# TensorE drains in the fused attention: who waits for a matmul's own increment, and who for a drain

## The chip, the core and the metric

The program runs on one core of one Trainium2 chip. Its five engines go by short names: PE (TensorE), DVE (VectorE), ACT (ScalarE), POOL (GpSimd) and SP (SyncE). They run their own instruction streams and meet only at semaphores: counters that one engine raises and another waits for. The metric is the device time of one execution in microseconds, the median of the runs shown.

## The reference, cut to what matters

Four graph layers follow one another on 3125 nodes of 256 features and 100,000 edges: an attention layer with two convolutions (L0), a dot-product attention (L1), a layer with edge features (L2), and another attention layer (L3). The change lies in the code that computes a convolution of L0 (twice) and the attention of L3:

```
h = (x @ W).reshape(-1, H, C)                     # H = 4 heads of 64
e = leaky_relu(alpha_s[src] + alpha_d[dst], 0.2)  # one score for an edge and a head
m = segment_max(e, dst);  ex = exp(e - m[dst])
alpha = ex / segment_sum(ex, dst)
out = segment_sum(h[src] * alpha[:, :, None], dst) + b
```

The edges are sorted by the node that receives them, so that each segment is a run of neighbours.

## The kernel before, in words

`attend` (line 1354) runs three times: for L0 with the tags `0a` and `0b`, for L3 without a tag. Tiles are named `at_..._0a`, `at_..._0b` and `at_...`. It takes the edges in units of 128; a turn is 16 units (STEP), in four quads of four (QUAD), and a stage has 51 turns. Every engine runs its own function `step` once a turn. There is no scheduler: instructions stand in the order of the code, and each engine goes down its list, stopping at waits.

A turn of step t, by engine:

- POOL gathers one unit's 128 rows from the node table in HBM with an indirect DMA (L1515), and fills a scratch tile after each one (`pause`, L1519). The ring holds three turns; a quad's gathers wait for that quad's matmuls two steps earlier.
- DVE scales a quad of gathered rows by their weights (`weigh_rows`, L1572); computes the scores (`y` at L1592 to `shrink`, a chain of some 17 short instructions); adds each unit's sums to the node's accumulator (`add`, L1566); and last `factor` (L1652), and at the head of the next step `rescale` (L1582). Its order is: rescale, rows of quad 0, scores, rows of quad 1, add 0 to 3, rows of quad 2, add 4 to 7, rows of quad 3, add 8 to 11, add 12 to 15, factor.
- ACT makes one-hot matrices (`hot`, `hot_r`), the exponents (`exp`), copies the turned exponents out of PSUM as weights (`alphas`, L1810), then `parts` (L1816), and `own` (L1835).
- PE runs scores, mm0 to mm11 (one matmul `mm{u}` for each unit, two passes each in the trace, L1680, into the four banks of `at_po`), 16 small `spread` matmuls (L1692), the exponents' transpose with `back_turned` as its last matmul (L1723, L1724), mm12 to mm15, eight matmuls on scratch (`keep_busy`, L107), and `joined` (L1735), whose result `own` needs.

Each engine has one semaphore that its instructions raise by position: `m.did("mm12", ...)` hangs an increment on the matmul, and `m.at("mm12", t)` is the value that the counter has by then, a register value in the loop. ACT waits before `alphas` at `m.at("back_turned", t)`, and DVE before each `add{u}` at `m.at("mm{u}", t)`. A matmul mm{u} waits for add{u-4}, which frees its bank.

Of the kernel before, what the change touches and what calls it, by code (L numbers as in the profile page):

```python
# [32 lines left out]
QUAD = 4  # L33
# [38 lines left out]
def gnn_kernel(nc, x_in, src_in, dst_in, attr_in, ew_in, W1, as1, ad1, b1, W2, as2, ad2, b2, Wq, bq, Wk, bk, Wv, bv,  # L72
# [30 lines left out]
    def keep_busy(eng, scratch, count):  # L103

        wide = scratch.shape[1] // P
        for _ in range(count):
            eng.matmul(scratch.rearrange("p (k n) -> p k n", n=P), ident16[:, :],  # L107
                       ident16[:, :].rearrange("p (k n) -> p k n", k=1).to_broadcast([P, wide, P]), start=True, stop=True)
# [1245 lines left out]
    def attend(tag, o, table, kind, scatter=0):  # L1354
# [26 lines left out]
        with ExitStack() as c:  # L1381
# [39 lines left out]
            ph = Phase()  # L1421
            vec, act, mat, fed, told, cleared = (ph.sem(n) for n in (
                "at_vector", "at_scalar", "at_tensor", "at_fed", "at_told", "at_cleared"))
# [4 lines left out]
            rows_in = [ph.sem(f"at_rows_in{h}") for h in range(2)]  # L1428
            v, s, m = Ops(vec, V, 3), Ops(act, A, 1), Ops(mat, M, 3)
            paused, blank = ph.sem("at_paused"), ph.sem("at_blank")  # L1430
            moving = Scatter(f"at_{tag}", ph, c, scatter) if scatter else None

            def run(eng, step):

                step(Turn(0, -1), False, False, True)
                step(Turn(0, 0), False, True, True)
                with eng.Fori(0, LAPS - 1) as i:
                    for k in range(1, BUFS + 1):
                        step(Turn(i, k), True, True, True)
                step(Turn(LAPS - 1, 1), True, True, True, True)  # L1440
                step(Turn(LAPS - 1, 2), True, True, False)
                step(Turn(LAPS - 1, 3), True, False, False, True)

            with nc.Block() as block:
# [86 lines left out]
                def _(eng):  # L1531
# [10 lines left out]
                    def step(t, sums, scores, spreads, short=False):  # L1542
# [15 lines left out]
                        def add(*us):  # L1558
                            for u in us:
                                if not sums or u >= quads * QUAD:  # L1560
                                    v.skip(f"add{u}")
                                    continue
                                eng.wait_ge(mat, m.at(f"mm{u}", t))
                                done("rescale" if u < 2 else f"add{u - 2}", t)
                                to = acc2[:, u % 2, bass.ds(gs[u], 1), 0:W]
                                v.did(f"add{u}", eng.tensor_tensor(to, to, po[:, u % 4:u % 4 + 1, 0:W], ALU.add))  # L1566
# [97 lines left out]
                @block.tensor  # L1664
                def _(eng):
                    def step(t, sums, scores, spreads, short=False):
                        a = t.plus(-1)
                        quads = TAIL if short and not scores else STEP // QUAD

                        def reduce(q):  # L1670
                            for j in range(QUAD):
                                u = q * QUAD + j
                                if not sums or q >= quads:
                                    m.skip(f"mm{u}")
                                    continue
                                if j == 0:
                                    eng.wait_ge(vec, v.at(f"rows{q}", t))
                                    eng.wait_ge(act, s.at(f"ext{q}", t))
                                eng.wait_ge(vec, v.at(f"add{u - 4}", t) if u >= 4 else v.at(f"add{u + 12}", a))
                                m.did(f"mm{u}", eng.matmul(po[:, u % 4, 0:W], hot[:, q % 2, j, :],  # L1680
                                                           rows[:, q % 2, j, :, :].rearrange("p h f -> p (h f)"),
                                                           start=True, stop=True))

                        def spread(h, gs):
                            if not spreads:
                                return m.skip(f"spread{h}")
                            eng.wait_ge(act, s.at(f"hot_r{h}", t))
                            if scores and h == 0:
                                eng.wait_ge(act, s.at("parts", a))
                            for k in range(HALF):  # L1690
                                u = h * HALF + k
                                mm = eng.matmul(pb[:, u, :, :].rearrange("p k c -> p (k c)"),  # L1692
                                                hot_r[:, h, k * P:(k + 1) * P],
                                                b_tab[:, bass.ds(gs[u], 1), :, 0:C].rearrange("p o k c -> p (o k) c"),
                                                start=True, stop=True)
                            m.did(f"spread{h}", mm)

                        if scores:
                            eng.wait_ge(act, s.at("picked", a))
                            if sums:  # L1700
                                eng.wait_ge(vec, v.at("y", a))
                            eng.sem_inc(told, 1)
                            m.did("scores", eng.transpose(scores_in, picked[:, :, :].rearrange("p h u -> p (h u)"), ident[:, :]))
                            keep_busy(eng, spare_b, 6)
                        else:
                            m.skip("scores")
                        reduce(0)
                        reduce(1)
                        reduce(2)
                        gs = None  # L1710
                        if spreads:
                            _, gs = nc.values_load_multi_w_load_instructions(
                                od["gof"][0:1, bass.ds((t.n + 1) * STEP, STEP)], engines=[ENG.PE], min_val=0, max_val=NB,
                                skip_runtime_bounds_check_because="the table is clamped to NB on the chip")
                        spread(0, gs)
                        spread(1, gs)
                        if scores:
                            if sums:
                                eng.wait_ge(vec, v.at(f"rows{quads - 1}", t))
                            eng.wait_ge(act, s.at("exp", t))  # L1720
                            eng.sem_inc(told, 1)
                            for k in range(KX):
                                eng.transpose(pe[:, k * R:(k + 1) * R], expd[:, k * P:(k + 1) * P], ident[0:R, 0:R])  # L1723
                            m.did("back_turned", eng.matmul(pe[:, KX * R:KX * R + H],  # L1724
                                                            expd[:, EX:EX + 1].to_broadcast([R, P]), ident[0:R, 0:R:STEP],
                                                            start=True, stop=True))
                        else:
                            m.skip("back_turned")
                        reduce(3)
                        if spreads:  # L1730
                            if scores:
                                keep_busy(eng, spare, 8)
                            eng.wait_ge(act, s.at("parts", t))
                            for k in range(3):
                                mm = eng.matmul(joined[0:C * STEP, :], parts[:, k, :, :].rearrange("p c u -> p (c u)"),  # L1735
                                                ident[:, :], start=(k == 0), stop=(k == 2))
                            m.did("joined", mm)
                        else:
                            m.skip("joined")

                    eng.sem_inc(mat, 2 * len(M))
                    run(eng, step)

                @block.scalar
                def _(eng):
                    done = lambda name, t: eng.wait_ge(act, s.at(name, t))

                    def step(t, sums, scores, spreads, short=False):
# [57 lines left out]
                        if scores:  # L1806
                            if sums and quads == STEP // QUAD:
                                done("ext3", t)
                            eng.wait_ge(mat, m.at("back_turned", t))
                            s.did("alphas", eng.activation(al[:, :, :, :].rearrange("p k h u -> p (k h u)"), pe[:, 0:KX * R],  # L1810
                                                           ACT.Copy))
                        else:
                            s.skip("alphas")
# [24 lines left out]
                        else:  # L1838
                            s.skip("own", *(["selfs"] if own_max else []))

                    run(eng, step)
            ph.end()

# [815 lines left out]
```

## Time and profile before

| | us |
|---|---|
| runs: 3, median | 7405.61 |
| lowest to highest | 7398.5 to 7406.8 |
| the profiled execution: its span, which is the only time it has | 8931.6 |
| POOL, PE, DVE, ACT busy in that span | 5847.5, 5412.5, 4963.7, 3871.5 |

The profiled execution took 1.206 times the median of the runs, so its times can't be taken for those of a plain run without thought. A duration of an ACT, DVE or POOL instruction is measured; a matmul's end is modelled. An engine's idle time before an instruction is shown with what ended it, where the profile can tell. Where it names a DMA of long before (`recs_s<-rnk_recs_now`), it could not tell.

### The profile page before, as it was taken

How to read it: one execution, taken by the hardware profiler on the slowest of the kernel's cores; microseconds unless marked ns; L12 is line 12 of the kernel's file. 1: busy time of each engine (PE TensorE's matmuls, PEld its weight loads, DVE VectorE, ACT ScalarE, POOL GpSimd, SP SyncE). 2: the span in 40 equal slices, each digit the busy share in tenths (PEclk: the TensorE clock that was granted, in tenths of full speed). 3: DMA queues.
4: the chain of work that ended last, by engine and by line, in shares of the span. 5: the costliest groups of instructions: out<-in, count | busy, mean ns of one | idle time of the engine just before them, and what ended most of it. 6: DMA issues, size and time to landing. Idle time of an engine off the chain costs nothing. (4 is left out here: it accounts for less than half of the span.)

```text
span 8931.6 us, 130458 instructions
## 1 busy us (share of the span) xinstructions
PE 5412.5 (61%) x23088; PEld 4000.6 (45%) x23089; DVE 4963.7 (56%) x11653; ACT 3871.5 (43%) x9075; POOL 5847.5 (65%) x8186
## 2 busy tenths in 40 slices
PE   6442365666535656664676666658888754666665
PEld 5431244444424444443455555435555533444443
DVE  6444355555545555554677777744444445555556
ACT  2220255455424554552244444335555533454444
POOL 0555677777747777775467666657777765777774
PEclk9555677777767777776788988868888866777777
DMA  4112233333313333331466666423333323333332
GB/s 143 49 49 52 75 95 95 95 96 95 86 44 97 96 95 95 96 97 33 127 176 178 177 176 175 129 64 99 100 101 100 101 53 101 99 99 99 98 98 74
DMA packets 580940, 894.72 MB, mean 100 GB/s; under 512 B 307359, under 2 KB 357708, under 8 KB 580448
## 3 DMA queue, kind: packets, MB, share of 16 engines
q0 software_dynamic: 245984, 649.30, 26.7%
q1 hardware_dynamic: 334448, 218.84, 8.9%
q10 hardware_dynamic: 416, 25.60, 0.9%
q8 instruction: 27, 0.44, 0.0%
q14 instruction: 65, 0.53, 0.0%
HBM read 859.36 MB, written 59.47 MB: 103 GB/s over the span
## 5 line engine op out<-in xcount | busy, mean ns | idle before, releaser
L2002 POOL DMA_INDIRECT ad_ring<-tab_qv,ad_idx x808 | 770.7, 954 | 506.4 <-issue 217.6
L1515 POOL DMA_INDIRECT at_ring_0a<-tab_s,at_idx_0a x808 | 774.3, 958 | 430.9 <-PE at_po_0a L1680 219.2
L2396 POOL DMA_INDIRECT ae_ring<-tab_a,ae_idx x808 | 777.9, 963 | 423.0 <-PE ae_po L2553 233.7
L1515 POOL DMA_INDIRECT at_ring_0b<-tab_s,at_idx_0b x808 | 772.8, 956 | 426.7 <-PE at_po_0b L1680 213.2
L1515 POOL DMA_INDIRECT at_ring<-tab_s,at_idx x808 | 780.1, 965 | 377.6 <-PE at_po L1680 183.0
L1680 PE MATMUL at_po_0a<-at_rows_0a,at_hot_0a 128*128 128x264 f32 x1616 | 625.6, 560 | 520.8 <-ACT at_hr_0a L1780 199.8
L1680 PE MATMUL at_po_0b<-at_rows_0b,at_hot_0b 128*128 128x264 f32 x1616 | 624.3, 559 | 512.2 <-ACT at_hr_0b L1780 201.7
L1680 PE MATMUL at_po<-at_rows,at_hot 128*128 128x260 f32 x1616 | 614.5, 553 | 444.5 <-DVE acc L1566 179.0
L1680 PEld LDWEIGHTS at_po_0a<-at_rows_0a,at_hot_0a 128*128 128x128 f32 x1616 | 439.3, 282 | 670.8 <-DVE acc L1566 262.0
L1680 PEld LDWEIGHTS at_po_0b<-at_rows_0b,at_hot_0b 128*128 128x128 f32 x1616 | 438.5, 282 | 662.4 <-DVE acc L1566 264.4
L1680 PEld LDWEIGHTS at_po<-at_rows,at_hot 128*128 128x128 f32 x1616 | 435.9, 280 | 586.2 <-DVE acc L1566 225.4
L2182 PE MATMUL ad_pk<-node_a,ad_hr 128*128 x1616 | 485.0, 452 | 337.6 <-issue 193.1
L2546 PE MATMUL ae_pM<-ae_we,ae_featT 64*128 64x256 f32 x1616 | 508.0, 465 | 171.3 <-issue 114.5
L1566 DVE TENSOR_TENSOR acc<-acc,at_po_0a 128x264 f32 x808 | 314.0, 422 | 483.9 <-PE at_po_0a L1680 215.1
L1566 DVE TENSOR_TENSOR acc<-acc,at_po_0b 128x264 f32 x808 | 312.9, 422 | 481.5 <-PE at_po_0b L1680 212.2
L566 POOL DMA_INDIRECT recs_s<-rnk_recs_now,rnk_pos_now x294 | 288.8, 982 | 409.9 <-DVE rnk_both L466 176.2
L2182 PEld LDWEIGHTS ad_pk<-node_a,ad_hr 128*128 128x128 f32 x1616 | 350.6, 226 | 452.2 <-issue 396.8
L1566 DVE TENSOR_TENSOR acc<-acc,at_po 128x260 f32 x808 | 307.1, 418 | 437.7 <-DMA recs_s<-rnk_recs_now,rnk_pos_now 178.8
L2553 PE MATMUL ae_po<-ae_msg,ae_hot 128*128 128x256 f32 x1616 | 464.8, 439 | 98.1 <-issue 60.9
L2506 DVE TENSOR_TENSOR ae_pre<-ae_ring,ae_pM 128x1024 f32<-128x1024 f32 x202 | 246.6, 1221 | 493.4 <-PE ae_pM L2546 187.7
L2546 PEld LDWEIGHTS ae_pM<-ae_we,ae_featT 64*128 64x128 f32 x1616 | 351.2, 229 | 314.6 <-issue 178.7
L2353 DVE TENSOR_TENSOR acc<-acc,ae_po 128x256 f32 x808 | 291.5, 416 | 297.9 <-PE ae_po L2553 218.8
(508 smaller groups left out, 14085.4 us busy)
## 6 DMA issues: line engine op xcount, KB each, us to landing
at_rr_0a<-relrow_d SPq DMA_DIRECT2D x102, 256.0 KB
at_rr_0b<-relrow_d SPq DMA_DIRECT2D x102, 256.0 KB
ad_rr<-relrow_d SPq DMA_DIRECT2D x102, 256.0 KB
at_rr<-relrow_s SPq DMA_DIRECT2D x102, 256.0 KB
ae_feat<-attr_pad SPq DMA_DIRECT2D x808, 32.0 KB
rnk_lrow<-lorow_f SPq DMA_DIRECT2D x98, 256.0 KB
attr_pad<-in_edge_attr_dram ACTq DMA_DIRECT2D x1, 25000.0 KB, 79.1
at_ring_0a<-tab_s,at_idx_0a POOLq DMA_INDIRECT x808
```

The source lines that it names most:

```text
L566: eng.indirect_dma_start(out=order["s"]["recs"], out_offset=bass.IndirectOffsetOnAxis(ap=pos_now[:, t.slot, k:k + 1], axis=0), in_=recs_no ...
L1515: eng.indirect_dma_start(out=ring[:, t.slot * STEP + u, :], out_offset=None, in_=table, in_offset=bass.IndirectOffsetOnAxis(ap=idx[:, t.sl ...
L1566: v.did(f"add{u}", eng.tensor_tensor(to, to, po[:, u % 4:u % 4 + 1, 0:W], ALU.add))
L1680: m.did(f"mm{u}", eng.matmul(po[:, u % 4, 0:W], hot[:, q % 2, j, :], rows[:, q % 2, j, :, :].rearrange("p h f -> p (h f)"), start=True, st ...
L2002: eng.indirect_dma_start(out=ring[:, t.slot * STEP + u, :], out_offset=None, in_=table, in_offset=bass.IndirectOffsetOnAxis(ap=idx[:, t.sl ...
L2182: mm = eng.matmul(pk[:, p % 2, (u % 2) * D:(u % 2 + 1) * D], hot_r[:, u // HALF, (u % HALF) * P:(u % HALF + 1) * P], k_tab[:, bass.ds(gs[u ...
L2353: own(eng.tensor_tensor(to, to, out_ps(q, j), ALU.add), False)
L2396: eng.indirect_dma_start(out=ring[:, k, :], out_offset=None, in_=table, in_offset=bass.IndirectOffsetOnAxis(ap=idx[:, k:k + 1], axis=0))\
L2506: own(eng.tensor_tensor(pre[:, q % 2, :, :].rearrange("p (a u) f -> p a (u f)", a=2), ring[:, q * QUAD:(q + 1) * QUAD, :].rearrange("p (a ...
L2546: mm = eng.matmul(pM[:, j // 2, (j % 2) * D:(j % 2 + 1) * D], featT[:, q % 2, j, :], We[:, :], start=True, stop=True)
L2553: mm = eng.matmul(po[:, (q % 2) * 2 + j // 2, (j % 2) * D:(j % 2 + 1) * D], hot[:, q % 2, j, :], msg[:, q % 2, j, :], start=True, stop=True)
```

## The change

Two semaphores are new. PE raises `turned_out` by a drain behind `back_turned`, and `summed_out` by a drain behind mm15 in every step that has sums. ACT's `alphas` waits for the first; DVE's add 12 to add 15 wait for the second, all four for the same value. The matmuls keep their own increments; other waits are as they were.

```diff
+            turned_out, summed_out = ph.sem("at_turned_out"), ph.sem("at_summed_out")
...
-                                eng.wait_ge(mat, m.at(f"mm{u}", t))
+                                if u < 3 * QUAD:
+                                    eng.wait_ge(mat, m.at(f"mm{u}", t))
+                                else:
+                                    eng.wait_ge(summed_out, t.n)
...
                             m.did("back_turned", eng.matmul(pe[:, KX * R:KX * R + H],
                                                             expd[:, EX:EX + 1].to_broadcast([R, P]), ident[0:R, 0:R:STEP],
                                                             start=True, stop=True))
+                            eng.drain().then_inc(turned_out, 1)
...
                         reduce(3)
+                        if sums:
+                            eng.drain().then_inc(summed_out, 1)
...
-                            eng.wait_ge(mat, m.at("back_turned", t))
+                            eng.wait_ge(turned_out, t.n + 1)
```

On DVE, at the end of a step in the loop, add 11 and add 12 stood as follows before. The list gives a semaphore's number by the name that first had it: `pads_blanked_1` is PE's counter, `consts_made_1` DVE's own.

```order
L1566 TENSOR_TENSOR acc<-acc,at_po_0a 128x264
L1563 REGISTER_ALU
L1532 REGISTER_ALU [waits pads_blanked_1]
L1566 ISA [waits consts_made_1]
L1566 TENSOR_TENSOR acc<-acc,at_po_0a 128x264
```

Now add 11 (the first three rows) and add 12 stand so:

```order
L1533 REGISTER_ALU [waits pads_blanked_1]
L1570 ISA [waits consts_made_1]
L1570 TENSOR_TENSOR acc<-acc,at_po_0a 128x264
L1533 REGISTER_ALU [waits at_summed_out_6]
L1570 ISA [waits consts_made_1]
L1570 TENSOR_TENSOR acc<-acc,at_po_0a 128x264
```

Each of the last four additions has lost the register instruction that made its wait's value, and waits for the drain behind mm15. On ACT, `alphas` stood so before (`set_chain_1` is ACT's own counter):

```order
L1770 ACTIVATE at_rows_0a<-at_al_0a 128x16x2 [waits pads_blanked_1]
L1746 REGISTER_ALU
L1809 REGISTER_ALU [waits set_chain_1]
L1810 ACTIVATE at_al_0a<-at_pe_0a 128x128 [waits pads_blanked_1]
L1815 REGISTER_ALU
```

And now:

```order
L1770 ACTIVATE at_hot_0a<-at_hot_0a,ones 128x512 [waits set_chain_1]
L1777 ACTIVATE at_rows_0a<-at_al_0a 128x16x2 [waits pads_blanked_1]
L1753 REGISTER_ALU
L1817 ACTIVATE at_al_0a<-at_pe_0a 128x128 [waits at_turned_out_6,set_chain_1]
L1822 REGISTER_ALU
```

One register instruction is gone there too, and the wait is for the drain behind `back_turned`.

## Rows read from the trace of the kernel before

**Rows 1.** The page: span, and the engines' busy time.

```profile
span 8931.6 us, 130458 instructions
PE 5412.5 (61%) x23088; PEld 4000.6 (45%) x23089; DVE 4963.7 (56%) x11653; ACT 3871.5 (43%) x9075; POOL 5847.5 (65%) x8186
```

**Rows 2.** Line 1592 (`y`): count, duration ns min/median/max, first and last start.

```profile
L1592 DVE TENSOR_TENSOR at_log_0a<-at_ta_0a,at_log_0a x51: 282/283/284, 1024.3 to 2490.3; 64x128 f32<-64x128 f32 x51
L1592 DVE TENSOR_TENSOR at_log_0b<-at_ta_0b,at_log_0b x51: 282/283/284, 2666.1 to 4124.0; 64x128 f32<-64x128 f32 x51
L1592 DVE TENSOR_TENSOR at_log<-at_ta,at_log x51: 282/283/284, 7475.7 to 8866.7; 64x128 f32<-64x128 f32 x51
```

**Rows 3.** Groups by line: busy us, mean ns; idle before, by releasers.

```profile
L1515 POOL DMA_INDIRECT at_ring_0a<-tab_s,at_idx_0a x808 | 774.3, 958 | 430.9 <-PE at_po_0a L1680 219.2 <-issue 143.9 <-DMA recs_s<-rnk_recs_now,rnk_pos_now 41.9
L1519 POOL MEMSET at_pause_0a<- 128x256 f32 x808 | 264.0, 327 | 0.4
```

**Rows 4.** Timeline of a turn with gathers: start us, us, instruction, idle before.

```profile
1540.29 0.33 PE L1724 MATMUL at_pe_0a<-ident,at_exp_0a 64*128 64x4 f32 x2
1540.55 2.68 PE L1680 MATMUL at_po_0a<-at_rows_0a,at_hot_0a 128*128 128x264 f32 x8
1543.04 0.28 ACT L1810 ACTIVATE at_al_0a<-at_pe_0a 128x128 f32<-128x128 f32 x1 [5.30 <-PE at_po_0a L1680]
1543.51 0.95 POOL L1515 DMA_INDIRECT at_ring_0a<-tab_s,at_idx_0a  x1 [0.17 <-issue]
1544.00 0.43 DVE L1566 TENSOR_TENSOR acc<-acc,at_po_0a 128x264 f32 x1 [5.31 <-PE at_po_0a L1680]
1544.95 0.95 POOL L1515 DMA_INDIRECT at_ring_0a<-tab_s,at_idx_0a  x1 [0.16 <-issue]
1545.53 0.43 DVE L1566 TENSOR_TENSOR acc<-acc,at_po_0a 128x264 f32 x1 [1.10 <-DMA recs_s<-rnk_recs_now,rnk_pos_now]
1546.97 0.43 DVE L1566 TENSOR_TENSOR acc<-acc,at_po_0a 128x264 f32 x1 [1.01 <-PE at_ta_0a L1703]
1548.41 0.43 DVE L1566 TENSOR_TENSOR acc<-acc,at_po_0a 128x264 f32 x1 [1.01 <-DMA recs_s<-rnk_recs_now,rnk_pos_now]
```

**Rows 5.** Timeline of the third stage's end: the last gather, then a turn without.

```profile
8838.37 0.96 POOL L1515 DMA_INDIRECT at_ring<-tab_s,at_idx  x1 [0.17 <-issue]
8845.56 0.28 DVE L1592 TENSOR_TENSOR at_log<-at_ta,at_log 64x128 f32<-64x128 f32 x1 [1.75 <-PE at_po L1680]
...
8857.44 1.43 DVE L1566 TENSOR_TENSOR acc<-acc,at_po 128x260 f32 x4
8860.02 0.33 PE L1724 MATMUL at_pe<-ident,at_exp 64*128 64x4 f32 x2
8860.28 2.02 PE L1680 MATMUL at_po<-at_rows,at_hot 128*128 128x260 f32 x8
8860.45 0.22 ACT L1810 ACTIVATE at_al<-at_pe 128x64 f32<-128x64 f32 x1 [2.53 <-PE at_pe L1724]
8861.14 1.76 DVE L1566 TENSOR_TENSOR acc<-acc,at_po 128x260 f32 x4 [2.27 <-PE at_po L1680]
8862.81 0.22 DVE L1652 TENSOR_SCALAR at_pe<-at_pe,notfirst_s 128x4 f32<-128x4 f32 x1
8864.44 0.27 ACT L1835 ACTIVATE at_log<-at_tt 64x128 f32<-64x128 f32 x1 [1.43 <-PE at_tt L1735]
8866.75 0.28 DVE L1592 TENSOR_TENSOR at_log<-at_ta,at_log 64x128 f32<-64x128 f32 x1 [1.74 <-ACT at_hot L1763]
```

**Rows 6.** PE's drains: at a stage's end without gathers, and among indirect DMAs.

```profile
8884.00 5.37 PE L1680 MATMUL at_po<-at_rows,at_hot 128*128 128x260 f32 x16 [2.80 <-DVE at_rows L1572]
L1444 PEldq DRAIN  x3: 1158/1182/1412, 2512.3 to 8888.3; - x3
825.93 5.59 PE L873 MATMUL un_pb<-un_reached,ones 25*128 25x392 f32 x8 [2.01 <-issue]
L664 PEldq DRAIN  x2: 998/6592/12187, 825.9 to 7441.7; - x2
```

## Prediction

> **What bounds the kernel now.** I read the page first [rows 1]: no engine is busy for more than 65% of the span, so waits set the time, not one engine's work. The change touches three stages, so next comes the length of a turn in them. `y` starts 51 times in a stage; first to last start, over 50 turns, is 29.3 us a turn in each of the first two stages and 27.8 in the third [rows 2], 28.8 on average. Then, who sets that pace. POOL's part is a gather of 0.958 us, a fill of 0.327 us, and about 0.16 us between [rows 3, 4]: 1.44 us from gather to gather, 23.1 us for 16. That leaves POOL 5.7 us a turn, and its largest wait is for PE's sums, 219 us in a stage [rows 3]. So in the profiled execution POOL follows, and a loop through PE, ACT and DVE leads.
>
> The timeline shows the loop. With gathers running, `back_turned` is over at 1540.62 (1540.29 + 0.33), yet `alphas` starts at 1543.04, 2.4 us late; mm12 to mm15 end at 1543.23, but their four additions start at 1544.00, 1545.53, 1546.97 and 1548.41, about 1.45 us apart, the distance of the gathers [rows 4]. In the third stage's end, where no gather runs any more, `alphas` starts 0.1 us after `back_turned` (8860.35 to 8860.45), the four additions run within 1.76 us, and a turn from `y` to `y` takes 21.2 us (8845.56 to 8866.75) [rows 5]. So PE's increments reach the others late while POOL gathers, and that is most of what a turn loses in the profile. The Trainium skill puts a matmul's increment at about 26 ns, one after another ("TensorE: Matmul & The Clock Gate", The cost: per-tile semaphore tail). The rows say 1.45 us among gathers, 50 times that, so the measurement decides; by the rule the drains could save under 0.1 us a turn.
>
> A plain run is 0.829 of the profiled span. Were a turn shortened alike, it would be 23.9 us (an estimate from rows 1 and 2): above POOL's 23.1, above the 21.2 without late signals. So a plain turn has room for 1 to 3 us of late signals, not for the 7 of the profile.
>
> **The change part by part.** All of it stands in one loop: `y`, exponents, mm4 to mm11, spread, `back_turned`, mm12 to mm15, add 12 to 15, factor, rescale, rows of quad 0, register loads, `y`. I sum what it adds to one turn; 50 turns a stage have add 12 to 15, so 150 in all.
>
> *Removed.* Four register instructions on DVE and one on ACT. Additions whose sums are there follow each other in 0.36 us (four in 1.43 [rows 5]), less than one addition's own 0.43 [rows 4]: the sequencer is already ahead, so these are worth nothing. A stall behind them would show as a gap between additions.
>
> *The additions wait for mm15 instead of for their own matmul.* Without late signals, mm15 ends at 8862.30 and the last addition at 8862.90, 0.60 us later: the additions went along with the matmuls [rows 5]. Now all four come after mm15: 1.43 us plus the 0.1 that a signal takes, so 1.53 behind mm15. That is +0.93 us. Behind them on DVE wait factor, rescale, the next rows and `y`; nothing covers it, since DVE goes down its list. What it releases late in PE (mm0 of the next turn, whose bank add 12 frees) waits for those rows anyway.
>
> *The first drain.* Behind it on PE stand mm12 to mm15, the scratch matmuls, `joined` and the next scores. A drain's length is seen at a stage's end: the third stage's last matmul ends at 8889.37, the drain (its first and last starts and its three lengths are in one row; 8888.3 + 1.16) at about 8889.4, within 0.1 us of it [rows 6]. Before, mm12's weights were loading at 8860.28, 0.07 us before `back_turned` ended [rows 5]; now they can't before the drain. Bounds: 0.05 us (a drain alone), and 2.5 us if it waits for late signals as `alphas` did [rows 4]. Not below nothing: PE's order is the same, with a stop in it. I take 0.12, the drain and the lost overlap.
>
> *The second drain.* It adds 0.05 to the wait of the additions. On PE it moves the scratch matmuls and `joined` by as much, or, if it lasts, by more; `own` is read by `y`, but is done at 8864.71, 2.0 us before it [rows 5]. That cover is lost only if both drains together hold PE for more than 2 us.
>
> *`alphas` waits for the drain.* It starts as late as the drain ends, 0.05 us more; behind it on ACT stand `parts`, `picked` and the next one-hots, and `rows` of the next turn wait for it no earlier than for `rescale`. Hidden.
>
> *SP and POOL* lose and gain no instruction; their DMAs wait for the same steps.
>
> Sum: 0.93 + 0.12 + 0.05 = 1.1 us a turn, 165 us in 150 turns. Made against the profiled span it is 8931.6 to about 9097; I carry the 165 us to the runs unscaled, since it consists of engine durations: 7405.6 + 165 = 7571. Ends of the sum: 1.03 us a turn (155 us) with the drains at their least, and up to 3.5 a turn (2.5 of the first drain among late signals, plus 0.93) or 525 us with them late.
>
> **The rivals.**
>
> *POOL's pace hides it.* If plain turns have no late signals, the loop is 21.2 us in the third stage, and 22.3 with the change, under POOL's 23.1. The first two stages have more work on the way (two transposes, and two columns of exponents), but hardly 0.8 us of it. Then the time stays: 7405, at most 15 us more. For it: the gathers' pace comes from one row, and the signals were late in an execution that was a fifth longer than a plain one. Against: by the 23.9 of above, a plain turn lies over POOL's pace.
>
> *Faster: the drain's own increment escapes the lateness.* What is late is the matmuls' increments; the drain's is another instruction's. If a drain ended 0.05 us after the last matmul even among gathers, `alphas` would start 2.3 us sooner in the turn at 1540, and the last addition at about 1544.5 instead of 1548.4 [rows 4], in the profile nearly 4 us. In plain runs a turn can fall from 23.9 to POOL's 23.1 and no further: 0.8 × 150 = 120 us, so about 7285. It decides where plain signals are later than the 1.1 us that the drains cost. The Trainium skill speaks for it: of a drain it says that the sequencer itself carries it out and pushes its update ("Perfetto Trace Analysis", Sequencer-only Instruction (DRAIN, etc)), apart from the engine's write acknowledgement; by that rule this rival holds, and no run here shows a drain in this place. Against it stands one drain among indirect DMAs: the matmuls before it end at 831.52 (825.93 + 5.59), and the drain, from 825.9 for 12.19 us, at 838.1, 6.6 us later; at a stage's end without DMAs that was under 0.1 [rows 6]. So a drain waits for whatever holds the matmuls' signals.
>
> *Much slower: the drains hold PE among gathers.* By that same pair of rows each drain waits as long as the signals are late, and now PE stands still meanwhile. Where mm12 started at 1540.55, it would start at 1543.0, so 2.5 us more, and then the second drain and four additions in a row: 3.5 us a turn. With half to all of that in plain runs: 260 to 525 us, so 7670 to 7930.
>
> **How the numbers follow.** My forecast (the loop leads, and gets 1.03 to 1.7 us longer: 7540 to 7660, likeliest 7571) has 0.5; POOL's pace hides it, 0.18; faster, 0.16; drains that hold PE, 0.16. The runs differ by 8 us among themselves, so less than 0.2%, 15 us, can't be told from no change. Faster by over 0.2% is the third case, 0.16. Within 0.2% is most of the second, 0.15. Slower has the rest, 0.69. The range goes from 7370, below the second case and taking in the upper end of the third, to 7760, which takes in the lower third of the fourth; about 0.12 and 0.08 stay outside. The forecast's own range is 7540 to 7660.
>
> **What would show it.** Right, if after the change the four last additions always stand in one run of about 1.43 us after mm15, a gap of 0.1 to 0.3 us lies on PE between `back_turned` and mm12 where no gather runs, and the turn without gathers goes from 21.2 to about 22.3. Drains that wait for late signals show as a gap of 2 us and more at mm12 among gathers, with `alphas` no earlier. The faster rival shows as `alphas` 0.1 to 0.2 us behind `back_turned` among gathers. POOL's pace shows as a turn of 23.1 with POOL's waits for PE gone. I am wrong in the step on lateness if the time falls, and in the claim that the loop leads if it stays.

## The result, and the profile after

The changed kernel takes 7677.8 us (median of 4 runs, 7675.37 to 7683.69), the kernel before 7403.93 in the same comparison: a ratio of 1.0373, with an interval of 1.0359 to 1.0387, or 274 us more. The page of the changed kernel:

```profile
span 7673.4 us, 130188 instructions
PE 5079.4 (66%) x23088; PEld 3742.4 (49%) x23089; DVE 4966.7 (65%) x11653; ACT 3884.7 (51%) x9075; POOL 5855.0 (76%) x8186
q14 instruction: 214, 1.75, 0.1%
```

Its span is that of its runs. The profile of before in [rows 1] was taken in a disturbed execution, 1.2 times as long as the runs, so from here on the kernel before is read in a second profile of it, the first experiment below, with a span of 7396.4 us. Line 1596 is now `y`; its three stages:

```profile
L1596 DVE TENSOR_TENSOR at_log_0a<-at_ta_0a,at_log_0a x51: 281/283/284, 846.9 to 2097.0; 64x128 f32<-64x128 f32 x51
L1596 DVE TENSOR_TENSOR at_log_0b<-at_ta_0b,at_log_0b x51: 281/282/284, 2250.6 to 3550.8; 64x128 f32<-64x128 f32 x51
L1596 DVE TENSOR_TENSOR at_log<-at_ta,at_log x51: 281/283/284, 6339.3 to 7605.9; 64x128 f32<-64x128 f32 x51
```

The same lines in the undisturbed profile of before:

```profile
L1592 DVE TENSOR_TENSOR at_log_0a<-at_ta_0a,at_log_0a x51: 281/283/284, 846.9 to 2037.2; 64x128 f32<-64x128 f32 x51
L1592 DVE TENSOR_TENSOR at_log_0b<-at_ta_0b,at_log_0b x51: 281/283/284, 2188.4 to 3378.8; 64x128 f32<-64x128 f32 x51
L1592 DVE TENSOR_TENSOR at_log<-at_ta,at_log x51: 281/283/285, 6165.1 to 7330.5; 64x128 f32<-64x128 f32 x51
```

First to last `y` grew by 60 us in stage 0a, 110 in 0b and 101 in the third, together 271 of the 274. The same edit stands in all three stages, so the extra 50 and 41 us of the last two need a cause of their own.

A turn among gathers in the undisturbed profile of before, answering to [rows 4]; each row gives the start, the length in us, the instruction and the idle time before it:

```profile
1578.42 0.33 PE L1724 MATMUL at_pe_0a<-ident,at_exp_0a 64*128 64x4 f32 x2
1578.69 2.05 PE L1680 MATMUL at_po_0a<-at_rows_0a,at_hot_0a 128*128 128x264 f32 x8
1578.77 0.95 POOL L1515 DMA_INDIRECT at_ring_0a<-tab_s,at_idx_0a  x1 [0.16 <-issue]
1578.79 0.28 ACT L1810 ACTIVATE at_al_0a<-at_pe_0a 128x128 f32<-128x128 f32 x1 [2.92 <-PE at_pe_0a L1724]
1579.63 1.78 DVE L1566 TENSOR_TENSOR acc<-acc,at_po_0a 128x264 f32 x4 [2.81 <-PE at_po_0a L1680]
```

PE's signals are not late: `alphas` starts 0.04 us behind `back_turned`, though POOL gathers, and the additions go along with mm12 to mm15. Two turns of the changed kernel, cut to the same places:

```profile
1490.00 0.33 PE L1728 MATMUL at_pe_0a<-ident,at_exp_0a 64*128 64x4 f32 x2
1490.66 3.53 PE L1684 MATMUL at_po_0a<-at_rows_0a,at_hot_0a 128*128 128x264 f32 x8 [0.33 <-issue]
1494.47 1.45 DVE L1570 TENSOR_TENSOR acc<-acc,at_po_0a 128x264 f32 x4 [5.92 <-PEq L1736]
...
1515.60 0.33 PE L1728 MATMUL at_pe_0a<-ident,at_exp_0a 64*128 64x4 f32 x2
1516.08 0.28 ACT L1817 ACTIVATE at_al_0a<-at_pe_0a 128x128 f32<-128x128 f32 x1 [3.02 <-PEq L1731]
1516.27 2.04 PE L1684 MATMUL at_po_0a<-at_rows_0a,at_hot_0a 128*128 128x264 f32 x8 [0.33 <-issue]
1518.59 1.45 DVE L1570 TENSOR_TENSOR acc<-acc,at_po_0a 128x264 f32 x4 [4.58 <-PEq L1736]
```

Between `back_turned` and mm12 PE stands for 0.33 us; `alphas` comes 0.15 us behind; the four additions are one run of 1.45 us, 0.28 us after mm15. And the same eight passes of mm12 to mm15 take 3.53 us in one turn and 2.04 in the next. The columns of a table by stretch (busy us of PE, PEld, DVE, ACT, POOL, granted clock, DMA share, GB/s) say why:

```profile
1490.70:1494.10 3.40, 3.40 (x8) 2.44 (x8) 0.00 (x0) 2.51 (x8) 3.08 (x5) 0.56 0.38 110
1516.30:1518.30 2.00, 2.00 (x8) 1.40 (x8) 0.00 (x0) 1.97 (x8) 1.84 (x3) 1.00 0.37 112
```

TensorE was granted 0.56 of its clock in the first, so 1.2 GHz for nearly nine tenths of it, and 2.4 GHz in the second. That term moves from kernel to kernel, and will matter below.

The third stage's end, the last turn from `y` to `y` (answering to [rows 5]):

```profile
7581.72 0.28 DVE L1596 TENSOR_TENSOR at_log<-at_ta,at_log 64x128 f32<-64x128 f32 x1 [1.75 <-PE at_po L1684]
7596.21 0.33 PE L1728 MATMUL at_pe<-ident,at_exp 64*128 64x4 f32 x2
7596.80 3.65 PE L1684 MATMUL at_po<-at_rows,at_hot 128*128 128x260 f32 x8 [0.25 <-issue]
7600.64 1.43 DVE L1570 TENSOR_TENSOR acc<-acc,at_po 128x260 f32 x4 [5.63 <-PEq L1736]
7605.92 0.28 DVE L1596 TENSOR_TENSOR at_log<-at_ta,at_log 64x128 f32<-64x128 f32 x1 [1.74 <-PE at_po L1684]
```

This turn takes 24.2 us; with the 2.02 us that these matmuls took in [rows 5], instead of 3.65, it would be 22.6, against 21.2 there. In the undisturbed profile of before the same turn, from 7307.60 to 7330.55, takes 22.95 us with 3.71 for these matmuls, so the change adds 1.25 to 1.4 us to it.

Last, the head of a step in the changed kernel: its line 1586, `rescale`, with what ended DVE's idle time before it in the whole span (us, times; "issue" is idle time that no wait in the profile explains), and then one case of the first kind.

```profile
  issue: 102.0, 30
  DVE at_pe_0a L1656: 18.6, 49
...
```

```profile
2739.14 0.23 DVE L1656 TENSOR_SCALAR at_pe_0b<-at_pe_0b,notfirst_d 128x4 f32<-128x4 f32 x1
2742.58 0.70 DVE L1586 TENSOR_TENSOR acc<-acc,at_pe_0b 128x528 f32 x1 [3.21 <-issue]
```

Thirty times DVE stood for about 3.4 us between `factor` and `rescale` and waited for nothing that the profile shows, 15 times in 0b, 15 in the third stage, never in 0a. `rescale` is the first thing behind the loop's jump, and a lap has three turns: one stall a lap. At the same time the queue that loads code (q14) carried 214 packets and 1.75 MB instead of 65 and 0.53.

### The profile page after: what moved, and what is told of

Same layout as the page of the kernel before. It is cut to its first block and busy times, and to the rows that moved or that the text cites. A ratio compares the mean times of both kernels' runs of the same rounds, so it can differ in the third digit from the quotient of the medians.

```text
span 7673.4 us, 130188 instructions
## 1 busy us (share of the span) xinstructions
PE 5079.4 (66%) x23088; PEld 3742.4 (49%) x23089; DVE 4966.7 (65%) x11653; ACT 3884.7 (51%) x9075; POOL 5855.0 (76%) x8186
## 3 DMA queue, kind: packets, MB, share of 16 engines
q14 instruction: 214, 1.75, 0.1%
## 5 line engine op out<-in xcount | busy, mean ns | idle before, releaser
L1684 PE MATMUL at_po_0b<-at_rows_0b,at_hot_0b 128*128 128x264 f32 x1616 | 570.3, 520 | 437.4 <-ACT at_hr_0b L1787 302.0
L1684 PE MATMUL at_po_0a<-at_rows_0a,at_hot_0a 128*128 128x264 f32 x1616 | 548.0, 504 | 410.6 <-ACT at_hr_0a L1787 314.2
L1684 PE MATMUL at_po<-at_rows,at_hot 128*128 128x260 f32 x1616 | 556.6, 511 | 386.2 <-DVE acc L1570 286.2
L1684 PEld LDWEIGHTS at_po_0a<-at_rows_0a,at_hot_0a 128*128 128x128 f32 x1616 | 392.9, 252 | 529.7 <-DVE acc L1570 344.5
L1684 PEld LDWEIGHTS at_po<-at_rows,at_hot 128*128 128x128 f32 x1616 | 397.6, 255 | 503.4 <-DVE acc L1570 310.6
L2189 PE MATMUL ad_pk<-node_a,ad_hr 128*128 x1616 | 412.3, 400 | 221.0 <-DVE ad_prod L2086 191.1
L2553 PE MATMUL ae_pM<-ae_we,ae_featT 64*128 64x256 f32 x1616 | 453.3, 426 | 97.4 <-DVE ae_pre L2513 97.4
L2189 PEld LDWEIGHTS ad_pk<-node_a,ad_hr 128*128 128x128 f32 x1616 | 303.9, 196 | 324.5 <-issue 285.8
L2288 ACT ACTIVATE ad_hot<-iota_row,ad_nrel 128x128 f32<-128x128 f32 x808 | 257.5, 389 | 377.8 <-PE ad_po L2227 377.8
L2227 PE MATMUL ad_po<-ad_ring,ad_hot 128*128 128x264 f32 x1616 | 433.1, 408 | 11.8 <-DVE acc L2065 4.8
```

Source lines behind the costliest of these rows:

```text
L2189: mm = eng.matmul(pk[:, p % 2, (u % 2) * D:(u % 2 + 1) * D], hot_r[:, u // HALF, (u % HALF) * P:(u % HALF + 1) * P], k_tab[:, bass.ds(gs[u ...
L2288: ins = eng.activation(hot[:, q % 2, j, :], iota_row[:, :], ACT.Abs, bias=nrel[:, of.slot, k:k + 1])
L2553: mm = eng.matmul(pM[:, j // 2, (j % 2) * D:(j % 2 + 1) * D], featT[:, q % 2, j, :], We[:, :], start=True, stop=True)
```

## The experiments

**The kernel before, once more**

No edit.

> The kernel before, unchanged, for a second profile: the first had a span 1.206 times the runs' median, the changed kernel's has none of that. If late increments of TensorE belong to the kernel (theory of the prediction), alphas starts 2 us and more behind back_turned among gathers here too, and the span is far above 7404. If they belonged to that one execution, the span is within 1% of 7404 and alphas starts 0.1 us behind back_turned throughout; the turns of the three stages are then 23.1 (POOL's pace) to 23.9. It also shows whether VectorE already stalls 3.2 us at rescale in every third turn, as the changed kernel does: 102 us in all there (theory: code loading), or has not more than 20 us.

7398.25 us, span 7396.4. The lateness of [rows 4] isn't there: the rows of before in the section above are from this run. Its code queue and its `rescale`:

```profile
q14 instruction: 65, 0.53, 0.0%
```

```profile
  DVE at_pe L1652: 23.3, 49
...
  issue: 0.3, 1
```

No stall of DVE is here, and so two things are to be told apart: the waits of the change, and the stalls.

**One half of the change at a time**

The first drain and the wait of `alphas`:

```diff
+                            eng.drain().then_inc(turned_out, 1)
...
-                            eng.wait_ge(mat, m.at("back_turned", t))
+                            eng.wait_ge(turned_out, t.n + 1)
```

> The first drain and ACT's wait for it alone; the additions wait for their own matmuls. By the sum: 0.12 us a turn, 18 us, ratio 1.002 (7405 to 7440). By the rival that the drain costs most: over 100 us, ratio over 1.013. VectorE's list is as before, so by the code theory there is no stall at rescale beyond that of the kernel before.

7449.23 us, ratio 1.0067 [1.005, 1.0083], so 49 us. No stalls.

The second drain and the wait of the additions:

```diff
+                        if sums:
+                            eng.drain().then_inc(summed_out, 1)
...
-                                eng.wait_ge(mat, m.at(f"mm{u}", t))
+                                if u < 3 * QUAD:
+                                    eng.wait_ge(mat, m.at(f"mm{u}", t))
+                                else:
+                                    eng.wait_ge(summed_out, t.n)
```

> The second drain and the four additions' wait for it alone; alphas waits for its matmul. By the sum 0.98 us a turn, 147 us (7550, 1.020), if VectorE does not stall at rescale; with that stall (code theory: VectorE's list is the changed kernel's) 240 to 255 us, 7645 to 7660, 1.033.

7549.45, ratio 1.0203 [1.0186, 1.022]: 149 us, in the span of the theory without stalls, but for the wrong reason: it has 30 stalls (98 us), so the wait itself shows only some 50 us, or up to 80 if they count no more than taking them away gives further down.

No drain; the four additions wait for mm15's own increment:

```diff
-                                eng.wait_ge(mat, m.at(f"mm{u}", t))
+                                eng.wait_ge(mat, m.at("mm15" if u >= 3 * QUAD else f"mm{u}", t))
```

> No drain; the four additions wait for mm15's own increment. By the sum 0.93 us a turn, 140 us (7545, 1.019). If instead the drain is what costs, under 30 us. VectorE's list is shorter than before by 27 instructions in all (by 36 in the changed kernel), so the stall at rescale may come or not: with it up to 100 us more, 7645.

7571.97, ratio 1.0229 [1.0212, 1.0246], about 170 us with 30 such stalls again, and in stage 0b 17 us more of such idle time ahead of the gathered rows (L1572), which the kernel with the drain doesn't have. Drain or increment makes little difference to the additions: the last one ends 1.72 us behind mm15 with the drain and 1.68 without. What counts is that all four wait for mm15. But the halves, without the stalls, cost 49 and 50 to 80 us, and the whole about 200. Where did the rest hide? The mean of 45 turns of stage 0a, where no kernel stalls, worked out from the traces:

```
us                              before  first  second  mm15  changed
y to back_turned's end           15.91  15.87   15.86 15.91   15.83
back_turned's end to mm12        -0.07   0.34   -0.07 -0.07    0.34
mm12 to mm15's end                2.86   2.63    2.05  2.04    2.88
mm15's end to last addition's     0.68   0.68    1.72  1.68    1.73
last addition's end to next y     4.46   4.47    4.33  4.33    4.33
turn                             23.84  23.99   23.89 23.89   25.11
```

The waits cost the same in each kernel that has them: +0.41 for the first drain, +1.04 behind mm15 (+1.00 without the drain), -0.13 after it. What hid them is the third line. With the second drain alone, mm12 to mm15 ran at 2.4 GHz in 45 of 45 turns; before, in 22 of 45. Three turns of it in a row, each with 2.05 us for the eight passes:

```profile
1514.19 2.05 PE L1684 MATMUL at_po_0a<-at_rows_0a,at_hot_0a 128*128 128x264 f32 x8
...
1538.39 2.05 PE L1684 MATMUL at_po_0a<-at_rows_0a,at_hot_0a 128*128 128x264 f32 x8
...
1562.14 2.05 PE L1684 MATMUL at_po_0a<-at_rows_0a,at_hot_0a 128*128 128x264 f32 x8
```

In the whole change that gain is gone again: 12 of 45 turns below 2.3 us.

Over the three stages the same means close the account. With the second drain alone mm12 to mm15 are 0.81, 0.82 and 0.16 us shorter than before, some 89 us in 150 turns, and the wait's 0.91 us a turn, 137 us, less these is 48. With the first drain alone they are 0.23 and 0.21 us shorter in 0a and 0b and 0.13 longer in the third stage, 15 us of the 61. In the whole change they are within 0.04 us of before, so nothing hides the 0.41 and 0.91: 198 us.

**Drains without the waits for them**

Both drains on PE; `alphas` and the additions wait as before.

```diff
+                            eng.drain().then_inc(turned_out, 1)
...
+                        if sums:
+                            eng.drain().then_inc(summed_out, 1)
```

> Both drains on PE, but every wait as before: alphas waits for back_turned's own increment, the four last additions for their own matmuls. Theory that a drain costs its stop on PE and the stall of DVE comes from DVE's changed code alone: DVE's list is that of before, so no stalls of 3 us ahead of rescale; the first drain's stop (0.33 us between back_turned and mm12 in the changed kernel) is the same as with the first drain alone, which cost 49 us, and the second drain has nothing late behind it: 7440 to 7460. Rival, that the waits and not the stops cost: within 15 us of 7404.

7441.63, ratio 1.0051 [1.0034, 1.0068], 39 us. Drains that nobody waits for cost what the first drain and its wait cost: a turn of 0a takes 23.96 us here and 23.99 there. So it is PE's stop and not the wait of `alphas`; the second drain's stop is not seen in the time.

**DVE's code moved, in the changed kernel and in the one before**

Unread increments ahead of DVE's steps in stage 0b, 24 in the changed kernel, 104 in the kernel before; nothing else.

```diff
+                    if tag == "0b":
+                        unused = ph.sem("at_unused")
+                        for _ in range(24):
+                            eng.sem_inc(unused, 1)
                     run(eng, step)
```

> The changed kernel, with 24 semaphore increments that nobody reads ahead of DVE's steps in stage 0b, so that the loops of stages 0b and the third end 24 instructions further on in DVE's code (the loop of 0b at the very place where it ends in the kernel before). Theory that 102 us of the 274 are DVE's wait for its code at the jump back: the 30 stalls of 3.2 to 3.4 us ahead of rescale go, the queue of the code loads moves a third as much, and the time falls by about 100 us to 7575. Rival, that the stalls come from the drains or the waits: the stalls stay, 7678 plus about 2 for the increments.

7606.21, ratio 1.0279 [1.0262, 1.0296]. All 30 stalls are gone and the code queue is at 65 packets; `rescale` in this run:

```profile
  DVE at_pe_0b L1656: 20.7, 49
  DVE at_pe L1656: 19.3, 49
  DVE at_pe_0a L1656: 18.9, 49
```

The time falls by 0.94% of the kernel before, 70 us, and not by the 102 of the stalls: a turn in 0b is 0.91 us shorter, in the third stage 0.77, where a third of a stall is 1.1 us. From the last addition to `y` it is 1.00 and 0.92 us shorter; mm12 to mm15 and the stretch up to `back_turned`'s end each got 0.04 to 0.09 longer.

> The kernel before, with 104 unread semaphore increments ahead of DVE's steps in stage 0b: if code comes in blocks of 128 instructions (1.75 MB in 214 packets is 8.2 KB a packet), this puts the ends of the loops of 0b and of the third stage at the place in a block where the changed kernel has them. Theory of the place in the code: stalls of about 3.3 us once in three turns, 15 in a stage, some or all of them visible: first two rows of the stage's turn from 23.85 to about 24.7 (part of a stall hides behind POOL's pace), 7404 plus 50 to 100 us: 7455 to 7505. Rival, that the stalls come from the change in waits or from the loop's length: 7404 plus about 5 for the increments.

7511.31, ratio 1.0147 [1.013, 1.0164]: 109 us more for 104 increments of no use, a few us above the range expected. The stalls of the changed kernel stand in the kernel before:

```profile
  issue: 105.6, 31
```

```profile
q14 instruction: 216, 1.77, 0.1%
```

From the last addition to `y` a turn is 0.92 and 0.86 us longer in the two stages, some 90 of the 109 us; most of the rest is mm12 to mm15, longer by 0.15 and 0.22.

Together these two settle it: the stalls come from where DVE's loop lies in its code, and neither from drains nor from waits. That code comes in blocks of 128 instructions was used to choose the 104, and one such number is no proof of the size.

**Does POOL's pace hide anything?**

```diff
-            pause = sb(f"at_pause_{tag}", [P, 2, QUAD, 2 * P], F32, c)
+            pause = sb(f"at_pause_{tag}", [P, 2, QUAD, P], F32, c)
```

> The kernel before with POOL's fill after each gather half as wide (128x128 instead of 128x256). Theory that in plain runs POOL's pace sets the first two stages (gather 0.959 + fill 0.328 + 0.2 between is 1.487 us, 23.8 a turn, and the turn is 23.84): the fill falls to about 0.2, POOL's pace to about 21.7, and the turn falls to the loop's own length, at most the 23.29 of the third stage: 0.5 to 1.0 us a turn in 100 turns, 7300 to 7355, the third stage as before. Rival, that the loop leads already: within 15 us of 7404.

7382.43, ratio 0.997 [0.9961, 0.998]. The turn of 0a stays at 23.85 us, and POOL's idle time goes up instead; of the 20 us gained, the three stages' turns hold some 5, and where the others lie is not shown. Stage 0b's gathers, in this run and then before (busy us, mean ns, idle before):

```profile
L1515 POOL DMA_INDIRECT at_ring_0b<-tab_s,at_idx_0b x808 | 774.4, 958 | 243.7 <-PE at_po_0b L1680 110.0
```

```profile
L1515 POOL DMA_INDIRECT at_ring_0b<-tab_s,at_idx_0b x808 | 774.9, 959 | 158.0 <-issue 107.1
```

My theory that POOL sets the first two stages fell: the loop leads at 23.85 us, and POOL, whose own work is nearly as long, follows.

**TensorE's clock, tried on both sides**

With the half-wide fill, ten scratch matmuls behind mm0 to mm3, where PE had been idle for 6.6 us; in the kernel before, and in the changed one with its 24 increments.

```diff
                         reduce(0)
+                        if scores and sums:
+                            for _ in range(10):
+                                eng.matmul(pb_bank[:, 2 * P:4 * P], ident[:, :], ident[:, :].rearrange("p (k n) -> p k n", k=1).to_broadcast([P, 2, P]), start=True, stop=True)
                         reduce(1)
```

> The kernel before with the half-wide fill, and with ten more scratch matmuls (f32, 128x128 by 256 columns, about 0.5 us each) behind mm0 to mm3, where PE stood idle for 6.6 us until mm4. Theory that TensorE's granted clock at mm12 to mm15 is a term of its own: their 8 passes take 2.05 us at 2.4 GHz (in stage 0a with the second drain alone) and 2.85 to 2.98 us on average in the kernel before, where part of the turns has 1.2 GHz there. If PE isn't idle ahead of them the clock stays up: 0.8 to 0.95 us a turn, 120 to 140 us less than the 7382 of the half-wide fill: 7240 to 7265. Rival, that their length isn't on the path or the clock doesn't follow PE's idle time: 7382 within 15.

7241.04, ratio 0.9787 [0.977, 0.9803]: faster than both kernels, and the number expected, but not at the place expected. First PE behind its idle time in the undisturbed kernel before, mm4 to mm11, with a granted clock of 0.50 in the first 3.8 us; then the end of one turn and the start of the next in this run:

```profile
1522.50 5.84 PE L1680 MATMUL at_po_0a<-at_rows_0a,at_hot_0a 128*128 128x264 f32 x16 [6.67 <-ACT at_hr_0a L1780]
```

```profile
1531.25 3.74 PE L1680 MATMUL at_po_0a<-at_rows_0a,at_hot_0a 128*128 128x264 f32 x8
...
1540.09 4.48 PE L1710 MATMUL at_pb_0a<-ident 128*128 128x256 f32 x20
1546.84 2.05 PE L1680 MATMUL at_po_0a<-at_rows_0a,at_hot_0a 128*128 128x264 f32 x8 [2.28 <-ACT at_hr_0a L1783]
```

Behind the scratch mm4 to mm7 run at 2.4 GHz, eight passes in 2.05 us, in this turn and in 32, 33 and 43 of 45 turns of the three stages; before, in one turn of all three together. `back_turned` ends 14.86 us after `y` instead of 15.91. That microsecond is the gain: the turn of 0a falls from 23.85 to 22.95 us. mm12 to mm15 still take 2.8 to 3.0 us on average in the three stages, here 3.74.

> The changed kernel with 24 unread increments ahead of stage 0b (no stalls at the jump), the half-wide fill and the same ten scratch matmuls. Theory of the clock: mm12 to mm15 fall from 2.95 to 2.05 us here too, and the two drains cost what their waits cost, whatever the clock: 1.04 us for the additions behind the drain and 0.41 us for the first drain, less 0.1 that the additions' shorter sequence gives back, 1.3 to 1.45 us a turn, so 195 to 220 us above the kernel before with the same scratch matmuls: about 7455. Rival, that the drains also hinder the clock: mm12 to mm15 stay near 2.9 us, and the distance grows to over 300 us.

7472.76, ratio 1.0098 [1.0081, 1.0115], 232 us above the one before with the same scratch, a little over the 195 to 220 expected. mm12 to mm15: 2.75, 2.66 and 3.10 us in the three stages, nearer to the rival's 2.9 than to 2.05, but the distance is not the rival's 300 us, so neither theory has both. The waits cost 0.41, 1.05 and -0.14 us a turn in 0a, as without the scratch. What differs lies ahead of them: mm4 to mm7 get 2.4 GHz in 18 and 21 of 45 turns of 0a and 0b, not in 32 and 33, and `back_turned` ends 15.17 us after `y` in 0a, 0.31 later than in the kernel above. The shorter mm12 to mm15 give 0.26 of that back. Why mm4 to mm7 have the lower clock here more often is not shown.

Then fourteen instead of ten, on both sides:

```diff
-                            for _ in range(10):
+                            for _ in range(14):
```

> As the kernel before with the half-wide fill and scratch matmuls, but with fourteen of them: ten took 4.48 us and left PE idle for 2.3 us ahead of mm4, so fourteen take 6.3 and leave 0.5. With ten, mm4 to mm11 went at 2.4 GHz in most turns and mm12 to mm15 did not (3.0, 2.8 and 3.0 us on average in the three stages, 2.05 at 2.4 GHz). Theory that the clock falls for want of work on PE ahead of it: with the gap closed mm12 to mm15 come to 2.05 to 2.3 us too, another 0.6 to 0.9 us a turn: 7105 to 7150. Rival, that the clock at mm12 to mm15 has nothing to do with that gap, or that the longer scratch delays mm4: 7241 or up to 50 us above.

7264.05, ratio 0.9804 [0.9788, 0.9821]. The gap ahead of mm4 is closed, the clock stays at 2.4 GHz up to mm11, and mm12 to mm15 are as slow as ever:

```profile
1511.74 6.21 PE L1710 MATMUL at_pb_0a<-ident 128*128 128x256 f32 x28
1518.62 2.05 PE L1680 MATMUL at_po_0a<-at_rows_0a,at_hot_0a 128*128 128x264 f32 x8 [0.68 <-ACT at_hr_0a L1783]
...
1526.44 3.63 PE L1680 MATMUL at_po_0a<-at_rows_0a,at_hot_0a 128*128 128x264 f32 x8
```

My theory fell, and with it the number expected of both kernels with fourteen: what stands in that gap decides the clock of mm4 to mm11, not that of mm12 to mm15.

> The changed kernel (24 unread increments ahead of stage 0b, half-wide fill) with the same fourteen scratch matmuls. Theory of two costs and one clock: with mm12 to mm15 at 2.4 GHz on both sides, the drains cost their waits alone: additions 1.04 us, first drain 0.41, less 0.1: 1.35 us a turn, 200 us above the kernel before with fourteen, so about 7305 to 7350. Rival, that PE's stops at the drains bring the clock down again: mm12 to mm15 stay at 2.6 us or more, and the distance grows beyond 250 us.

7508.1, ratio 1.0137 [1.012, 1.0154]: 244 us above its partner. mm12 to mm15 take 3.31, 3.27 and 3.19 us here against 3.09, 3.00 and 3.12 there; less these 0.22, 0.27 and 0.07, its turns of 24.59, 24.55 and 23.84 stand 1.33, 1.38 and 1.36 us above the partner's 23.04, 22.90 and 22.41. With the clock of mm4 to mm11 equal on both sides, the waits cost some 1.35 us in all three stages; reckoned alike without scratch they cost 1.26 to 1.37. The clock adds its own.

## Why the prediction was right, and where it was not

*Direction and size of the waits: right, with luck in the total.* Slower by 1.1 us a turn was forecast, 165 us. Without the stalls, the changed kernel is 204 us slower (7606 against 7402), 1.36 us in each of 150 turns, inside the forecast's own range of 7540 to 7660. The measured 7678 is above that range. It lies in the wide one, and in that of the rival whose drains wait for late signals, because the stalls, which were in no sum, added 70 us. The lower end has a slip, too: 1.03 us in 150 turns gives 7560, not 7540.

*The additions behind mm15: right, 0.98 forecast with the second drain.* Measured +1.04 from mm15's end to the last addition's, of which 0.13 comes back before the next `y`: 0.91. They stand in one run of 1.45 us, as said. The second drain's own 0.05 is 0.04: the additions start 0.28 us behind mm15 with it and 0.24 when they wait for mm15's increment, so the additions alone are 0.87, where 0.93 was forecast. That 0.8 us of this cost would be hidden by the clock in some kernels was in no term.

*The first drain: mis-sized.* "I take 0.12, the drain and the lost overlap": it is 0.41. The drain itself ends 0.05 us behind the matmul's modelled end (the median of 153), but mm12 starts 0.33 us behind `back_turned`, where it had started 0.07 us ahead of its end. The bound of 0.05 from a stage's end [rows 6] priced the drain, and not PE's new start behind it, which no row of before shows.

*`alphas`: right.* It comes 0.1 us later and costs nothing that is seen, since drains without its wait cost as much.

*The removed register instructions: the step that failed.* "These are worth nothing" was drawn from the pace of the additions. They do follow each other as closely as before, in 1.45 us, but the term left out that taking them away moves DVE's code. That is 30 stalls of 3.4 us; taking them away by moving the code gave 70 us of the 274, and putting them into the kernel before cost 109. My range held the time with this in it, but no rival had it.

*The lateness of PE's signals: wrong for a plain run.* It was in one execution; I carried "room for 1 to 3 us of late signals" over from it. The sum didn't rest on it, two rivals did: there was nothing for a drain to escape (faster), and no late signal for it to wait out (much slower). Whether a drain would escape such lateness stays open, since no execution after the first had it. The Trainium skill gives a matmul's increment about 26 ns ("TensorE: Matmul & The Clock Gate", The cost: per-tile semaphore tail). The undisturbed trace agrees with that in size, since `alphas` starts 0.04 us behind the matmul's modelled end; the disturbed one doesn't, and I had let that one decide.

*POOL's pace hides it: wrong.* With a shorter fill POOL only waits longer.

*The turn without gathers* was to go from 21.2 to about 22.3; at equal clock it is 22.6. The changed kernel with its code moved shows it directly: 22.55 us, with 1.99 for mm12 to mm15.

*Open:* why mm12 to mm15 get 2.4 GHz in every turn of stage 0a with the second drain alone, and in about half before and a quarter after. There mm8 to mm11 already have it, with 2.02 us instead of 2.65. Idle time on PE ahead of mm4 was tried, and filling it did not raise the clock of mm12 to mm15 in the kernel before.

## What to carry to other kernels

Price a wait by what is queued behind it from the last producer's end to the next turn's start, and do it in an undisturbed execution: an execution much longer than the runs can show waits that plain runs don't have. When an edit changes the number of instructions on an engine whose loop is long, look at the idle time behind the jump and at the code queue before explaining the time by the edit. When halves don't add up to the whole, compare the same instructions' durations between the kernels: here, in stage 0a with the second drain alone, the clock hid 0.8 us of 1.0.

## What the runs showed of the hardware

A loop of DVE's code cost 3.1 to 4.0 us a lap or nothing, depending on where it lay: 150 more packets on the code queue, 109 us for 104 idle instructions.

A drain on PE ended with the matmuls (the additions stand 0.28 us behind mm15 with it, 0.24 without), but the next matmul started later: mm12 stood 0.33 us behind the first drain's matmul, and the scratch matmuls 0.11 us behind mm15 at the second, where both had overlapped. Cheap for those who wait for it, dearer for PE.

Ten useless matmuls in an idle gap of PE made the kernel before 2% faster (0.9787 with the shorter fill, which alone is 0.997), since the work behind the gap then ran at 2.4 GHz: mm4 to mm7 took 2.27 us on average in stage 0a instead of 3.88.
